# Scores and value products in one stretch each, and a new order of work on four engines, in a layered attention kernel

## The chip, the cores and the metric

The kernel runs on one core of a Trainium2 chip. The core has five engines that run their own instruction streams and meet only at semaphores: TensorE (PE for its matrix products, PEld for its weight loads), VectorE (DVE), ScalarE (ACT), GpSimd (POOL) and SyncE (SP, which issues the DMA transfers here). The metric is the device time of one execution in microseconds (us). Of the kernel before there are three runs, 1416.37, 1417.46 and 1418.73 us, and one profiled execution.

## The reference, cut to what matters

There are 16 sequences of 256 tokens with 256 channels. First comes a cross attention to a short context, then two layers of the kind below. The change touches the two layers alone.

```python
def _layer(x, wqkv, qs, ksc, wo, lg, lb, w1, b1, w2, b2):
    h = shift_token(x)                     # half of the channels come from the token before
    q, k, v = heads(h @ wqkv)              # 8 heads of 64
    q, k = rotary_xpos(l2norm(q) * qs, l2norm(k) * ksc)
    o = local_attention(q, k, v)           # windows of 128 tokens, each sees itself and the one before
    x = x + o @ wo
    h = layernorm(shift_token(x)) * lg + lb
    a, g = split(h @ w1 + b1)              # 2 * 682 columns
    return x + (a * gelu(g)) @ w2 + b2
...
x = x + xattn(layernorm(x), ctx)
x = x + ffn(layernorm(x))                  # two such layers
```

## The kernel before, in words

A step of the layer part handles one sequence of one layer, an item. There are 32 items, and the part is a pipeline written by hand: in step g the engines work on four items at once. In `run_l` they are called a (item g: projections to q, k and v, rotation and norms of q and k), b (item g-1: scores, softmax, value products, output projection), c (item g-2: layer norm and the hidden layer) and d (item g-3: the second product of the hidden layer). Steps 0 to 2 and 32 to 34 lack some of the four. Step 0 runs beside the end of the cross attention, step 33 and the rest finish the last item.

Every engine's `run_l` is a list of calls, and the order of that list is the order of its instructions. Nothing is scheduled by a tool. Each call waits on counters of the other engines (`at(b, 6, j)` is the count when piece j of item b is done), which guard data and also the reuse of the eight PSUM banks of `pb`; the tables `S_BANK`, `PT_BANK`, `QT_BANK`, `W1_BANK` say which bank a piece uses.

Names that matter here:

- `project(a, ..., t, part)`: six products of 512 columns, token tile t (0 or 1), part 0 q, 1 k, 2 v. `square` (ACT) and `squares` (DVE) form the norms, `rotate` (DVE) the two rotated parts, `add_parts`, `inverse_norms` and `norm_qk` (POOL) add them, take the inverse square root, and scale. `turn_qk` (PE) transposes the outcome and `copy_qk` (ACT) puts it into `qk_t`.
- `scores(..., j)`: j is 0, 1 or 2, and each makes two of the six softmax units u of item b. Their products have 64 rows (one head), and two heads share the array. `maxes` (DVE, with the mask), `exps` (ACT), `inverse_sums` and `norm_probs` (DVE, the division by the sum), `turn_p` (PE, transposes) and `probs_copy` (ACT) follow for each unit.
- `weigh(..., j)`: value products of units 2j and 2j+1, with 64 output columns each. `out_hi` (ACT) and `out_lo` (DVE) split the result into two parts, `out_product` (PE) multiplies by wo, `residual` (DVE) adds x. SP then moves one row down (`shift_down`), and `stats_h` (DVE) waits for that transfer.
- `turn_h`, `scale_h`, `split_h_hi`, `split_h_lo`, `hidden(..., m)`, `gelu`, `gate`, `gate_hi` (a cast), `gate_lo` (POOL): the hidden layer in six chunks m. `feed(..., k)` is its second product and `second_residual` adds it.
- `idle_products` are transposes whose result nobody reads. Before, 48 of them stand in step 1.

All matrix products but the scores, the value products and the transposes are sums of three products of parts (high and low), hence the threefold rows in the trace.

## Time and profile before

| | |
|---|---|
| median of 3 runs | 1417.46 us |
| the profiled execution's own time | 1418.17 us |
| its span, first to last instruction | 1416.2 us |
| granted clock of TensorE, mean | 0.999 |
| PE busy | 1384.4 us (98%) |
| PEld busy | 1239.3 us (88%) |
| DVE busy | 1097.6 us (78%) |
| ACT busy | 936.0 us (66%) |
| POOL busy | 783.8 us (55%) |

A row of the timeline reads: start, duration, engine, line, operation, output and inputs, shape, number of instructions, and in brackets the idle time ahead of it with what ended it. Products overlap, so the duration of one is longer than the distance to the next; what a product costs PE is the distance between the starts. A row of several instructions spans all of them. A row of the table by stretch reads: stretch, its length, busy time of PE, PEld, DVE, ACT and POOL with the number of instructions of each, the granted clock, the DMA engines' busy share, GB/s. Step 1 begins at 263.39 us, step 2 at 297.83, step 3 at 332.90, step 32 at 1362.08.

### The profile page before, as it was taken

How to read it: one execution, taken by the hardware profiler on the slowest of the kernel's cores; microseconds unless marked ns; L12 is line 12 of the kernel's file. 1: busy time of each engine (PE TensorE's matmuls, PEld its weight loads, DVE VectorE, ACT ScalarE, POOL GpSimd, SP SyncE). 2: the span in 40 equal slices, each digit the busy share in tenths (PEclk: the TensorE clock that was granted, in tenths of full speed). 3: DMA queues.
4: the chain of work that ended last, by engine and by line, in shares of the span. 5: the costliest groups of instructions: out<-in, count | busy, mean ns of one | idle time of the engine just before them, and what ended most of it. 6: DMA issues, size and time to landing. Idle time of an engine off the chain costs nothing.

```text
span 1416.2 us, 32821 instructions
## 1 busy us (share of the span) xinstructions
PE 1384.4 (98%) x11563; PEld 1239.3 (88%) x11563; DVE 1097.6 (78%) x3003; ACT 936.0 (66%) x2662; POOL 783.8 (55%) x640
## 2 busy tenths in 40 slices
PE   8999999989999999999999999999999999999998
PEld 7998998778888888888888888888888888888887
DVE  5777776668788788888888888788888888888874
ACT  6877767456666666666666667666666666666662
POOL 1212221646666666666666768766666666666643
PEclk9999999999999999999999999999999999999999
DMA  5223122101111001101111111111111111111101
GB/s 190 90 92 110 47 69 90 47 20 29 30 29 30 24 28 28 30 28 31 30 31 30 63 30 37 31 37 38 37 37 37 38 36 40 36 36 36 30 30 31
DMA packets 50517, 63.42 MB, mean 45 GB/s; under 512 B 8402, under 2 KB 32104, under 8 KB 50408
## 3 DMA queue, kind: packets, MB, share of 16 engines
q1 hardware_dynamic: 50408, 61.99, 14.0%
q8 instruction: 65, 1.06, 0.3%
q14 instruction: 44, 0.36, 0.1%
HBM read 38.17 MB, written 16.78 MB: 39 GB/s over the span
## 4 chain that ended last, share of the span: by engine, by line
PE 71%; DVE 12%; ACT 9%; issue 3%; DMA 2%; POOL 1%; SPq 1%; DVEq 0%; ACTq 0%; POOLq 0%
PE pb L568 34%; PE pb L881 7%; PE pb L895 6%; PE pb L857 6%; PE pb L826 6%; PE pb L841 5%; ACT x_p L1080 4%; PE pb L921 4%; ACT x_pt L1086 2%; DVE p_t L1593 1%; DMA x<-x 1%; DMA x_in<-x 1%; DVE p_t L1607 1%; DVE r_sin L1580 1%; ACT p_t L1223 1%
## 5 line engine op out<-in xcount | busy, mean ns | idle before, releaser
L1824 POOL TENSOR_TENSOR r_cos<-r_cos,r_sin 128x1024 f32<-128x1024 f32 x64 | 154.0, 2407 | 206.0 <-DVE r_sin L1580 206.0
L1223 ACT ACTIVATE p_t<-p_t,s_nm 128x128 f32<-128x128 f32 (+1 forms) x512 | 227.0, 445 | 25.9 <-DVE s_nm L1593 24.8
L568 PE MATMUL pb<-h_hi,w_hi 128*128 128x256 f32 x704 | 207.5, 295 | 1.5 <-DVE h_lo L1557 0.7
L568 PE MATMUL pb<-h_hi,w_lo 128*128 128x256 f32 x704 | 198.7, 282 | 0.0
L568 PE MATMUL pb<-h_lo,w_hi 128*128 128x256 f32 x704 | 198.6, 282 | 0.0
L1819 POOL TENSOR_TENSOR n_inv<-n_cl,half_neg 128x16 f32<-128x16 f32 x64 | 188.0, 2937 | 5.3
L1214 ACT ACTIVATE pt_t<-pb 128x512 f32<-128x512 f32 x192 | 113.8, 594 | 94.3 <-PE pb L841 93.8
L1607 DVE TENSOR_TENSOR p_t<-p_t,s_inv 128x512 f32<-128x512 f32 x192 | 173.4, 917 | 2.2
L568 PE MATMUL pb<-wqkv_hi,xt_hi 128*128 128x512 f32 x384 | 163.8, 427 | 3.6 <-DVE r_sin L1580 3.1
L1179 ACT ACTIVATE qk_sq<-pb 128x512 f32<-128x512 f32 x128 | 72.5, 592 | 142.9 <-PE pb L568 141.5
L1593 DVE CUSTOM_DVE_ANT_0 p_t<-pb,mask_t 128x128 f32<-128x128 f32 (+1 forms) x512 | 151.9, 353 | 16.9 <-PE pb L826 16.5
L1855 POOL TENSOR_TENSOR hg_lo<-hg,hg_hi 128x256 fp32r<-128x256 f32 (+1 forms) x192 | 142.1, 760 | 34.7 <-DVE hg_hi L1624 34.7
L568 PE MATMUL pb<-wqkv_lo,xt_hi 128*128 128x512 f32 x384 | 152.0, 396 | 0.0
L568 PE MATMUL pb<-wqkv_hi,xt_lo 128*128 128x512 f32 x384 | 150.7, 393 | 0.0
L568 PEld LDWEIGHTS pb<-h_hi,w_hi 128*128 128x128 f32 x704 | 134.0, 190 | 9.1 <-issue 6.4
L568 PEld LDWEIGHTS pb<-h_lo,w_hi 128*128 128x128 f32 x704 | 134.5, 191 | 0.0
L568 PEld LDWEIGHTS pb<-h_hi,w_lo 128*128 128x128 f32 x704 | 134.1, 191 | 0.0
L1831 POOL TENSOR_TENSOR r_cos<-r_cos,n_inv 128x1024 f32<-128x1024 f32 x64 | 123.4, 1929 | 5.0
L841 PE MATMUL pb<-ones_at,p_t 128*128 128x128 f32 x768 | 114.3, 279 | 5.0 <-DVE p_t L1607 4.3
L826 PE MATMUL pb<-qk_t 64*128 64x128 f32 (+1 forms) x1024 | 109.8, 343 | 1.3 <-DVE s_nm L1593 0.9
L1080 ACT ACTIVATE x_p<-pb,x_nm 128x77 f32<-128x77 f32 x256 | 79.2, 338 | 43.6 <-DVE x_nm L1375 43.6
L1202 ACT ACTIVATE gl<-pb,b_t 128x256 f32<-128x256 f32 x160 | 75.9, 475 | 46.3 <-PE pb L568 45.0
(145 smaller groups left out, 3920.7 us busy)
## 6 DMA issues: line engine op xcount, KB each, us to landing
y_state<-x SPq DMA_DIRECT2D x32, 256.0 KB, 2.0
x_cur<-y_state SPq DMA_DIRECT2D x32, 256.0 KB, 2.6
x_res<-y_state SPq DMA_DIRECT2D x32, 256.0 KB, 2.8
x_in<-x SPq DMA_DIRECT2D x16, 256.0 KB, 2.9
x_state<-x SPq DMA_DIRECT2D x16, 256.0 KB, 2.0
x_orig<-x_state SPq DMA_DIRECT2D x16, 256.0 KB, 2.9
out<-x SPq DMA_DIRECT2D x16, 256.0 KB, 2.2
x<-x SPq DMA_DIRECT2D x32, 112.0 KB, 2.3
```

What stands on the lines that cost most here:

```text
L568: mm = pe.matmul(dst, s, m, start=(n == 0 and k == 0), stop=(n == len(pairs) - 1 and k == 2))
L826: mm = pe.matmul(pb[:, S_BANK[u], k * keys:k * keys + keys], qk_t[r:r + DH, 0, ch, q_cols], qk_t[r:r + DH, 1, ch, 0:keys], start=True, sto ...
L841: mm = pe.transpose(pb[:, PT_BANK[u], k * P:k * P + P], p_t[:, u, k * P:k * P + P], id_f)
L1080: e = nc.scalar.activation(x_p[:, u, k, :], pb[:, 2 + u % 2, k * P:k * P + CTX], ACT.Exp, bias=x_nm[:, u, k:k + 1], scale=1.0, accum_out=x ...
L1214: nc.scalar.activation(pt_t[:, u % 4], pb[:, PT_BANK[u]], ACT.Copy).then_inc(act_pt, 1)
L1223: e = nc.scalar.activation(pu, pu, ACT.Exp, bias=s_nm[:, j, k:k + 1], scale=-1.0, accum_out=s_sum[:, j, k:k + 1])
L1593: e = nc.vector.tensor_tensor_reduce(p_t[:, j, k * keys:k * keys + keys], pb[:, S_BANK[j], k * keys:k * keys + keys], m, -1.0, FAR, ALU.ad ...
L1607: nc.vector.tensor_tensor(pu, pu, s_inv[:, u, 0:heads].unsqueeze(2).broadcast_to([P, heads, 512 // heads]), ALU.mult).then_inc(dve_pn, 1)
L1819: nc.gpsimd.tensor_tensor(n_inv[:, t], n_cl[:, t], half_neg[:], ALU.pow).then_inc(pool_inv, 1)
L1824: nc.gpsimd.tensor_tensor(r_cos[:, t], r_cos[:, t], r_sin[:, t], ALU.add).then_inc(pool_sum, 1)
L1831: nc.gpsimd.tensor_tensor(rows, rows, n_inv[:, t].unsqueeze(2).broadcast_to([P, 2 * HEADS, DH]), ALU.mult).then_inc(pool_qk, 1)
L1855: nc.gpsimd.tensor_tensor(hg_lo[0:rows, m], hg[0:rows, m], hg_hi[0:rows, m].bitcast(F32), ALU.subtract).then_inc(pool_hglo, 1)
```

## The change

It edits the order of the layer part on PE, ACT, DVE and POOL, with the banks and waits that go with it.

- PE: the three `scores` calls of a step stand directly behind each other, and so do the value products, now `weigh_late(0)`, `weigh_early`, `weigh_late(1)`. A step begins with `project(0, 1)`; `turn_next` and both halves of `out_product` move to the rear.
- `probs_copy` writes the transposed units back into `p_t` instead of a buffer of four (`pt_t` is gone), so `maxes` of the next item waits for the value products (`pe_av`) and no longer for the transposes.
- DVE, ACT, POOL: lists rewritten; `stats_h` goes from behind the second `maxes` to the rear of the step before. `gate(c, 0)` stands ahead of `rotate(a, 1)`.
- The idle products of step 1 are removed (16 in step 32 and 42 in step 0 stay), and the splitting of the second layer's wqkv goes in the order k, q, v.

```diff
-        S_BANK = [3, 4, 3, 4, 3, 4]
-        PT_BANK = [5, 7, 5, 7, 5, 2]
+        S_BANK = [2, 7, 3, 4, 5, 6]
+        PT_BANK = [5, 7, 5, 7, 4, 7]
...
+            def weigh_early(b, par):
+                pe.wait_ge(act_pt, at(b, UNITS, UNITS))
...
             def probs_copy(b, u):
                 act.wait_ge(pe_pt, at(b, UNITS, u + 1))
-                if u == 4:
-                    act.wait_ge(pe_av, at(b, 3, 1))
-                elif u in (0, 2) and later(b):
-                    act.wait_ge(pe_av, at(plus(b, -1), 3, 3 if u == 0 else 2))
-                nc.scalar.activation(pt_t[:, u % 4], pb[:, PT_BANK[u]], ACT.Copy).then_inc(act_pt, 1)
+                nc.scalar.activation(p_t[:, u], pb[:, PT_BANK[u]], ACT.Copy).then_inc(act_pt, 1)
...
# PE, run_l, a full step, new order (conditions left out)
+   project(0, 1); scores(0); scores(1); scores(2); project(0, 0)
+   feed(0); feed(1); turn_h; project(0, 2); feed(2); feed(3); feed(4)
+   turn_p(0); project(1, 0); feed(5); project(1, 1); project(1, 2)
+   turn_p(1); hidden(0); hidden(1); turn_p(2); turn_p(3); turn_p(4); hidden(2); turn_p(5)
+   weigh_late(0); weigh_early; weigh_late(1); hidden(3); turn_next
+   out_product(0); out_product(1); hidden(4); turn_qk(0); turn_qk(1); hidden(5); turn_qk(2); turn_qk(3)
...
# ACT, run_l, a full step, new order
+   square(0, 1); exps(0); exps(1); square(0, 0); scale_h; exps(2); copy_v(0); exps(3); exps(4)
+   probs_copy(0); square(1, 0); square(1, 1); exps(5); probs_copy(1); copy_v(1); gelu(0)
+   probs_copy(2) to (5); out_hi(0); gelu(1); out_hi(1); x_hi; gelu(2); gelu(3); gelu(4)
+   copy_qk(0); copy_qk(1); gelu(5); copy_qk(2); copy_qk(3)
...
# POOL, run_l, a full step, new order
+   gate_lo(d, 1) to (d, 4); deviation(c); gate_lo(d, 5); inverse_norms(0); add_parts(0); inverse_norms(1)
+   norm_qk(0); add_parts(1); kept_rows(c); gate_lo(c, 0); norm_qk(1)
```

On PE a step of before has three stretches of scores. The third stands between `feed` and `turn_p` (L881 and L841; L568 here the projections):

```order
L881 MATMUL pb<-w_hi,hg_hi 128x256
L881 MATMUL pb<-w_lo,hg_hi 128x256
L881 MATMUL pb<-w_hi,hg_lo 128x256
L826 MATMUL pb<-qk_t 128x128 x8
L841 MATMUL pb<-ones_at,p_t 128x128 x4
L568 MATMUL pb<-wqkv_hi,xt_hi 128x512
```

In the changed kernel all scores of a step stand between two projections (L840 scores, L571 the projections, L947 `turn_qk` of the step before):

```order
L947 MATMUL pb<-ones_at,r_cos 128x128 x8
L571 MATMUL pb<-wqkv_hi,xt_hi 128x512
L571 MATMUL pb<-wqkv_lo,xt_hi 128x512
L571 MATMUL pb<-wqkv_hi,xt_lo 128x512
L571 MATMUL pb<-wqkv_hi,xt_hi 128x512
L571 MATMUL pb<-wqkv_lo,xt_hi 128x512
L571 MATMUL pb<-wqkv_hi,xt_lo 128x512
L840 MATMUL pb<-qk_t 128x256 x8
L840 MATMUL pb<-qk_t 128x128 x8
L571 MATMUL pb<-wqkv_hi,xt_hi 128x512
```

Two changes of tile shape and back are gone from the step. (A row of the program is two in the trace for these products.)

The value products of before on PE, the first of their two stretches, with the transposes around it (L582 `turn_x`, L841 `turn_p`):

```order
L841 MATMUL pb<-ones_at,p_t 128x128 x8
L582 MATMUL pb<-ones_at,x_cur 128x128 x4
L857 MATMUL pb<-pt_t,v_t 64x128 x8
L841 MATMUL pb<-ones_at,p_t 128x128 x4
L568 MATMUL pb<-h_hi,w_hi 128x256
```

And in the changed kernel, one stretch behind the last `turn_p` (L857; L872 `weigh_late`, L884 `weigh_early`):

```order
L857 MATMUL pb<-ones_at,p_t 128x128 x4
L872 MATMUL pb<-p_t,v_t 64x128 x8
L884 MATMUL pb<-p_t,v_t 64x128 x8
L872 MATMUL pb<-p_t,v_t 64x128 x8
L571 MATMUL pb<-h_hi,w_hi 128x256
```

All of them now follow the last transpose, so the middle one has the copy of the last unit close ahead of it.

On DVE, before, the last division of a step follows the second rotation and the squares (L1574, L1580 `rotate`, L1563 `squares`, L1607 `norm_probs`):

```order
L1574 TENSOR_TENSOR r_cos<-pb,cos_t 128x512 [waits act_sq]
L1574 TENSOR_TENSOR r_cos<-pb,cos_t 128x512
L1580 TENSOR_TENSOR r_sin<-pb,sin_t 128x16x32 x2
L1563 TENSOR_REDUCE n_sq<-qk_sq 128x16 [waits pool_cl,act_sq]
L1601 RECIPROCAL s_inv<-s_sum 128x4 [waits act_exp]
L1607 TENSOR_TENSOR p_t<-p_t,s_inv 128x512 [waits dve_rec]
```

In the changed kernel the four last divisions (L1633) stand ahead of that rotation (L1600, L1606; L1589 `squares`):

```order
L1589 TENSOR_REDUCE n_sq<-qk_sq 128x16 [waits pool_cl,act_sq]
L1633 TENSOR_TENSOR p_t<-p_t,s_inv 128x512 [waits dve_rec] x2
L1627 RECIPROCAL s_inv<-s_sum 128x4 [waits act_exp] x2
L1633 TENSOR_TENSOR p_t<-p_t,s_inv 128x512 [waits dve_rec] x2
L1643 SCALAR_TENSOR_TENSOR hg<-pb,b_t,gl 128x256 [waits pool_hglo,act_gelu]
L1600 TENSOR_TENSOR r_cos<-pb,cos_t 128x512 [waits act_sq]
L1600 TENSOR_TENSOR r_cos<-pb,cos_t 128x512
L1606 TENSOR_TENSOR r_sin<-pb,sin_t 128x16x32 x2
```

So the divisions have moved ahead of the rotation, for which the sum of the rotated parts on POOL waits.

## Rows read from the trace of the kernel before

**Rows 1.** Busy by stretch: steps 1, 2, 3-31, one full step, step 32, 4 us.

```profile
263.39:297.83 34.44, 30.73 (x234) 25.66 (x232) 20.25 (x57) 18.07 (x53) 16.20 (x8) 0.95 0.08 26
297.83:332.90 35.07, 32.35 (x255) 27.32 (x255) 28.02 (x78) 22.06 (x60) 21.97 (x17) 1.00 0.08 20
332.90:1362.08 1029.18, 1024.21 (x8292) 915.15 (x8291) 836.35 (x2293) 686.36 (x1777) 664.89 (x500) 1.00 0.11 34
940.07:975.20 35.13, 35.13 (x287) 31.54 (x287) 28.84 (x79) 23.31 (x61) 22.47 (x18) 1.00 0.12 38
1362.08:1387.80 25.72, 22.29 (x205) 19.39 (x205) 14.91 (x56) 15.50 (x46) 2.53 (x4) 1.00 0.13 41
290.00:294.00 4.00, 4.00 (x33) 3.67 (x30) 1.29 (x2) 1.09 (x2) 2.77 (x2) 0.68 0.02 4
```

**Rows 2.** Timeline of PE around two stretches of scores in a full step.

```profile
945.34 0.28 PE L881 MATMUL pb<-w_hi,hg_lo 128*128 128x256 f32 x1
945.55 1.13 PE L826 MATMUL pb<-qk_t 64*128 64x256 f32 x8
946.61 0.50 PE L568 MATMUL pb<-wqkv_hi,xt_hi 128*128 128x512 f32 x1
946.95 0.40 PE L568 MATMUL pb<-wqkv_lo,xt_hi 128*128 128x512 f32 x1
...
951.72 1.16 PE L826 MATMUL pb<-qk_t 64*128 64x128 f32 x16
952.82 0.66 PE L841 MATMUL pb<-ones_at,p_t 128*128 128x128 f32 x4
```

**Rows 3.** Timeline of PE around the value products, and one copy on ACT.

```profile
957.63 0.60 PE L582 MATMUL pb<-ones_at,x_cur 128*128 128x128 f32 x4
958.16 1.09 PE L857 MATMUL pb<-pt_t,v_t 128*64 128x128 f32 x16
959.19 0.66 PE L841 MATMUL pb<-ones_at,p_t 128*128 128x128 f32 x4
...
964.41 0.60 PE L841 MATMUL pb<-ones_at,p_t 128*128 128x128 f32 x4
964.94 1.97 PE L857 MATMUL pb<-pt_t,v_t 128*64 128x128 f32 x32
966.84 0.39 PE L568 MATMUL pb<-h_hi,w_hi 128*128 128x256 f32 x1
...
965.04 0.60 ACT L1214 ACTIVATE pt_t<-pb 128x512 f32<-128x512 f32 x1
```

**Rows 4.** Timeline of DVE and POOL: divisions beside the power and beside the sum.

```profile
951.78 1.28 DVE L1607 TENSOR_TENSOR p_t<-p_t,s_inv 128x512 f32<-128x512 f32 x2
...
962.49 1.79 DVE L1607 TENSOR_TENSOR p_t<-p_t,s_inv 128x512 f32<-128x512 f32 x1
...
951.34 2.93 POOL L1819 TENSOR_TENSOR n_inv<-n_cl,half_neg 128x16 f32<-128x16 f32 x1
...
961.33 2.40 POOL L1824 TENSOR_TENSOR r_cos<-r_cos,r_sin 128x1024 f32<-128x1024 f32 x1 [4.93 <-DVE r_sin L1580]
```

**Rows 5.** Timeline of DVE: the residual and the statistics behind the shift.

```profile
940.17 0.69 DVE L1531 TENSOR_TENSOR x<-pb,x_res 128x512 f32<-128x512 f32 x1 [1.03 <-PE pb L895]
...
944.32 0.76 DVE L1537 BATCH_NORM_STATS2 l_st<-x 128x6 f32<-128x256 f32 x2 [1.44 <-DMA x<-x]
```

**Rows 6.** Groups by line and shape: maxes, rotation, squares, power, scaling.

```profile
L1819 POOL TENSOR_TENSOR n_inv<-n_cl,half_neg 128x16 f32<-128x16 f32 x64 | 188.0, 2937 | 5.3
...
L1831 POOL TENSOR_TENSOR r_cos<-r_cos,n_inv 128x1024 f32<-128x1024 f32 x64 | 123.4, 1929 | 5.0
...
L1593 DVE CUSTOM_DVE_ANT_0 p_t<-pb,mask_t 128x256 f32<-128x256 f32 x256 | 93.0, 420 | 16.6 <-PE pb L826 16.5
...
L1574 DVE TENSOR_TENSOR r_cos<-pb,cos_t 128x512 f32<-128x512 f32 x128 | 81.7, 680 | 3.3 <-ACT qk_sq L1179 3.1 <-issue 0.2
...
L1563 DVE TENSOR_REDUCE n_sq<-qk_sq 128x16 f32<-128x1024 f32 x64 | 77.6, 1213 | 0.0
```

More of the change, by code:

```diff
@@ L366, in qkv_bank @@
         def qkv_bank(a, t, part):
[L367 removed]
+            return (FIRST_BANK if is_first(a) else QKV_BANK)[t, part]
         def xt_bank(n):
@@ L941, in run_l @@
                     return
-                if isinstance(g, int) and g == 1:
-                    idle_products(5, 7)
+                if isinstance(g, int) and g == ITEMS:
+                    scores(a, b, c, d, 0)
+                    scores(a, b, c, d, 1)
+                    scores(a, b, c, d, 2)
+                    feed(b, c, d, 0)
+                    feed(b, c, d, 1)
+                    feed(b, c, d, 2)
+                    feed(b, c, d, 3)
+                    feed(b, c, d, 4)
+                    turn_p(a, b, d, 0)
+                    feed(b, c, d, 5)
+                    idle_products(16, 1)
+                    turn_h(b, c)
+                    turn_p(a, b, d, 1)
+                    hidden(a, b, c, 0)
+                    turn_p(a, b, d, 2)
+                    turn_p(a, b, d, 3)
+                    hidden(a, b, c, 1)
+                    turn_p(a, b, d, 4)
+                    turn_p(a, b, d, 5)
+                    weigh_late(a, b, c, was, 0)
+                    weigh_early(b, was)
+                    weigh_late(a, b, c, was, 1)
+                    hidden(a, b, c, 2)
+                    out_product(b, 0)
+                    out_product(b, 1)
+                    hidden(a, b, c, 3)
+                    hidden(a, b, c, 4)
+                    hidden(a, b, c, 5)
+                    return
@@ L984, in run_l @@
+                if c is not None:
+                    hidden(a, b, c, 2)
+                if b is not None:
+                    turn_p(a, b, d, 5)
+                if b is not None:
+                    weigh_late(a, b, c, was, 0)
+                    weigh_early(b, was)
+                    weigh_late(a, b, c, was, 1)
+                if c is not None:
+                    hidden(a, b, c, 3)
                 if has_next(a):
-                    turn_next(a, b, c)
+                    turn_next(a)
@@ L1259, in run_l @@
                     exps(b, 1)
+                if a is not None and not is_first(a):
+                    square(a, 0, 0)
+                if c is not None:
+                    scale_h(c, layer)
+                if b is not None:
                     exps(b, 2)
@@ L1309, in run_l @@
                     copy_qk(a, 1)
+                if c is not None:
+                    gelu(c, 5, layer)
+                    next_weights(g, 2)
+                if a is not None:
                     copy_qk(a, 2)
```

469 lines of the change are left out of this document (226 added, 243 removed).

## Prediction, on record before the changed kernel was run

> **What bounds the kernel now.** I first read the busy time by stretch [rows 1]. A full step takes 35.13 us and PE is busy in all of it, at full clock, while DVE has 28.84 us of work, ACT 23.31 and POOL 22.47. The 29 steps 3 to 31 take 1029.18 us; at 35.13 each they would take 1018.8, so 10.4 us are irregular waits. A step of the layers is therefore as long as PE's own list, and a gain must come out of what that list costs on PE, not out of a wait. Only steps 1 and 2 differ: step 1 lasts 34.44 us although it has neither hidden layer nor second product, and the clock is 0.95 in it, so it is made of waits and of idle products. Then I read PE's timeline for the distance between starts where the kind of product changes [rows 2, 3].
>
> **What a stretch of small tiles costs on PE.** Scores use 64 rows, value products 64 columns, all else the full array. Value products: 16 take 958.16 to 959.19, 1.03 us, and 32 take 964.94 to 966.84, 1.90 us [rows 3]. So 16 more cost 0.87, a pair 0.109, and every stretch has 0.16 us on top. Ahead of it four transposes take 0.53 us (957.63 to 958.16), where their own distance, (0.60 - 0.27) / 3 = 0.11, makes 0.44: 0.09 for the way in (0.27 is taken as the length of a single one). The first row behind lasts 0.66 against 0.60 for the same transposes elsewhere: 0.06 for the way out. Together 0.31 us for a stretch. Scores of 256 columns: four pairs at twice 0.109 would be 0.87, they take 1.06 (945.55 to 946.61), so 0.19; the way in is 945.34 to 945.55, 0.21 against about 0.12 for such a product (256 columns, half of the 0.23 to 0.24 of 512), 0.09; the first projection behind lasts 0.50 against 0.40, 0.10 [rows 2]. Together 0.38. The third stretch (128 columns, eight pairs) takes 1.10 against 0.87, 0.23, plus 0.09 and 0.06: 0.38.
>
> The change leaves one stretch of scores of three and one of value products of two. It saves 0.38 + 0.38 + 0.31 = 1.07 us a step. No product is added or taken out, and eight groups of transposes instead of seven cost nothing by rows: four take 0.44 with their way out. I put back 0.1 for what a change between the two score shapes may cost, which no row shows (between 0 and another 0.38). A full step then takes 35.13 - 0.98 = 34.15 us, if PE never waits.
>
> The Trainium skill says in "TensorEngine Tiling", section Key Properties, that changing the tiling mode drains TensorE while changing the tile alone does not. The 0.31 and 0.38 us are what this case's trace shows of it; by the page a switch between 64-row scores of two widths would cost nothing, which would make the step 34.05 us.
>
> **Does PE wait in the new order?** I laid the other engines' lists beside PE's new one, 0 being a step's first projection. PE then reaches scores at 1.6, the second projection at 4.4, `turn_h` 7.3, `turn_p(0)` 11.3, `turn_p(1)` 16.2, hidden 16.6, `turn_p(5)` 22.3, values 22.8 to 25.6, `out_product` 27.5 to 30.4, `turn_qk` 31.8.
>
> - Divisions on DVE. A division beside POOL's power takes 0.64 (two in 1.28 us, 951.78, POOL busy 951.34 to 954.27); beside the sum it takes 1.79, and it ends 0.55 after the sum does (962.49 to 964.28, sum until 963.73) [rows 4]. So the full-width POOL operations hold DVE's division or cast back until they end, the narrow power does not. In the new order DVE does the first division and the split of h while POOL does the power of tile 0, and four divisions in the power of tile 1. The second one follows the rotation without a break, so DVE starts it before POOL has seen the rotation. 1.1 us of blocking goes, but off PE's path.
> - DVE from the first maxes at 2.9: five maxes 3.6 us (0.35 for each of 256 keys, 0.42 with its end), `norm_h` 0.65, squares 1.15, two divisions 1.2, split 1.1, rotation 2.4 (four of 0.60), residual 0.6, last maxes 0.9, and 0.6 of reciprocals and waiting, 12.2 in all (maxes, squares and rotation by [rows 6], divisions by [rows 4], the others set equal to their like). It ends at 15.1, hidden needs it at 16.6: 1.5 spare.
> - The last unit: `turn_p(5)` starts at 22.3; its copy ends 1.3 later (before: 964.41 to 965.64, 1.23). `weigh_early` comes 0.53 for the transposes and 0.9 for the first 16 value rows later, 1.4. Some 0.15 spare, the tightest place.
> - POOL's last scaling: squares of tile 1 end at 16.8, power and clamp 3.7, scaling 1.9, sum 2.4 (after a wait for the rotation), kept rows and one `gate_lo` 2.1, scaling 1.9: 29.4 against 31.8.
> - ACT copies the last q/k tile by 0.8 of the next step; scores need it at 1.6.
> - The statistics, now at DVE's rear, wait for the shift. The residual starts at 31.7 at the latest, and from its start to the statistics it was 4.15 us (940.17 to 944.32) [rows 5]: 35.9, which is 1.7 of the next step, plus 1.0 of work: 2.7, just ahead of the maxes at 2.9. Nothing is lost.
>
> So steps 3 to 31 take 29 x 34.15 = 990.4 us, plus irregular waits. Half of the old 10.4 us stays, I estimate, since the long waits there fall where the new order has 1 us of spare, but the split of wqkv and w1 now stands ahead of work that is late: 5 us. 995.4 against 1029.18: -33.8.
>
> **Steps 1, 2 and 32.** In step 1 PE waits for others. New order: first division 8.5 us in, projections of tile 1 end at 13.2, squares of tile 1 at 13.8; then POOL alone is the chain: clamp and power 3.7, scaling 1.93, sum 2.4, scaling 1.93 [rows 4, 6], 23.8, and 16 transposes 1.8: 25.7 us against 34.44, -8.7. In the old order the last division stands behind a rotation, squares and the sum, and the second `out_product` behind everything. Step 2 lacks the second product, 32 x 0.12 = 3.8 us, and waits 1.4 us for its first division: 31.8 against 35.07, -3.3. Step 32 has no projection: scores wait 1.1 us for the q/k copies and, since `scale_h` stands ahead of `exps(2)` on ACT, the softmax waits for `turn_h` at 10. The residual comes 28.5 us in and not 26.0: +2.5. What is behind it keeps its length.
>
> **Sum.** 1418.17 - 33.8 - 8.7 - 3.3 + 2.5 = 1374.9 us, by the profiled execution, which is 0.7 above the median of the runs. I forecast 1375 us, -3.0%.
>
> **Rivals.**
>
> - A short wait in every step, at the value products (0.15 spare) or at the scores (0.8 spare). For: the two smallest margins, and no row shows the copies in this order. 0.3 to 0.6 us a step, 29 times: 1384 to 1392.
> - Joining saves only part: the 0.19 and 0.23 us inside a stretch are not its beginning but the pace of its pairs. For: the pair at 256 columns is only inferred. Then 0.42 us a step less is gained, 1387, and with a wait on top up to 1400.
> - The clock. Without the 48 idle products PE of step 1 pauses some 1 us at a time. The clock was 0.68 in 290 to 294 [rows 1], behind a pause of 2.5 us; there the row of 32 value products took longer than its 1.97. At half clock for 4 us the loss is 2 us: 1377. The skill's page "TensorE: Matmul & The Clock Gate", section What's actually happening, says that an idle engine falls to the lower level; the trace agrees at that place.
> - **Slower: the statistics at DVE's rear become the loop.** Shift, statistics, maxes, ..., last maxes, hidden, `out_product`, residual, shift is a closed ring through every step. It has 0.2 + 1.5 = 1.7 us of spare at a shift of 3.5 us. Each us beyond lengthens all steps. Break-even is a step of 35.64 us (29 x 35.64 + 5 = 1029.18 + 9.5), a shift of 6.7 us. At 7.2, from other transfers of SP beside it, a step is 36.15 and the time 1433. For: DVE idles for this transfer in every step now. Against: 3.5 us [rows 5].
> - **Slower by a rule.** If POOL's power of 2.94 us [rows 6] blocked DVE as the sum does, the split of h in the new order would end 3.2 us late, hidden 1.7 us late, a step would take 35.85, and the time would be 1424. Divisions take 0.64 us beside it [rows 4], so no. The skill's "SBUF — State Buffer", section SBUF: two separate sides, says that whichever of a GpSimd operation and a VectorE one with two SBUF inputs starts first holds the shared ports to its end; the trace agrees for the sum, not for the power.
> - The order moves but the step stays 35.1: only steps 1, 2 and 32 gain, 1409.
>
> **How the numbers follow.** Forecast 0.58 (1366 to 1384), short wait 0.18, joining saves part 0.09, clock 0.04, step stays 0.03, ring 0.05, rule 0.01, 0.02 for anything else that ends within 0.2%. Range 1364 to 1398: below, both open costs at nothing and no irregular wait; above, into part-saving with a wait. 0.2% is about what the runs can tell from no change. Faster 0.92, same 0.02, slower 0.06.
>
> **What would show it.** Right: a full step of 34.1 to 34.3 us, PE busy in all of it; one row of scores of some 2.8 us and one of value products of 2.8; step 1 near 26 us, step 32's residual 28 us in. Wrong: idle time of PE ahead of `weigh_early` on ACT's copy, or ahead of hidden on the maxes; DVE idle at the statistics for more than 1 us; a division of 1.7 us; a row of scores of 3.2 us.

## The result and the profile after

| | before | after |
|---|---|---|
| median of the runs | 1417.54 us (1416.37 to 1418.73, 4 runs) | 1372.26 us (1371.82 to 1373.79, 4 runs) |
| ratio after : before | | 0.9686, 95% interval 0.9675 to 0.9698 |
| span of the profiled execution | 1416.2 us | 1371.6 us |
| granted clock, mean | 0.999 | 0.996 |
| PE busy | 1384.4 us | 1343.5 us (98%) |
| DVE busy | 1097.6 us | 1033.0 us (75%) |
| POOL busy | 783.8 us | 797.3 us (58%) |

The change makes the kernel 3.1% faster, 45 us; the forecast was 1375 us. The table by stretch answers [rows 1]: length of the stretch, then busy time of PE, PEld, DVE, ACT and POOL, granted clock, DMA share, GB/s. The stretches are step 1, step 2, steps 3 to 31, one full step, step 32 up to the last residual, and the last residual to the end.

```profile
263.54:289.55 26.01, 23.35 (x187) 19.21 (x185) 18.60 (x59) 17.53 (x53) 15.70 (x8) 1.00 0.13 34
289.55:321.75 32.20, 30.78 (x257) 27.53 (x256) 26.48 (x77) 22.07 (x62) 22.40 (x16) 1.00 0.09 24
321.75:1315.08 993.33, 990.60 (x8293) 914.89 (x8292) 776.01 (x2295) 689.39 (x1779) 678.90 (x499) 1.00 0.12 35
973.30:1007.42 34.12, 34.12 (x289) 31.55 (x288) 26.57 (x80) 23.51 (x62) 22.98 (x17) 1.00 0.13 38
1315.08:1342.71 27.63, 23.83 (x218) 22.69 (x219) 14.34 (x57) 16.11 (x47) 2.86 (x4) 0.94 0.10 33
1342.71:1371.60 28.89, 21.68 (x164) 20.93 (x162) 14.61 (x34) 5.28 (x11) 10.88 (x15) 0.94 0.13 38
```

Steps 3 to 31 gave 35.9 us (1029.18 to 993.33), step 1 8.4, step 2 2.9. The last part, from the scores of step 32 to the end, lasts 56.5 us against 54.1: 2.4 lost. 25 of the 29 steps last 34.12 us, each PE's list without a pause; step 18 lasts 36.79 and holds most of what is irregular. Of the 35.9 us, 29 x 1.01 = 29.3 are the shorter full step; the other 6.6 are irregular waits that went (10.4 before, 3.8 now).

PE's timeline of that full step, at the places of [rows 2, 3]. Columns: start, length, engine and line, operands, tile and shape, count.

```profile
974.87 2.89 PE L840 MATMUL pb<-qk_t 64*128 64x256 f32 x32
977.69 0.50 PE L571 MATMUL pb<-wqkv_hi,xt_hi 128*128 128x512 f32 x1
...
995.49 0.60 PE L857 MATMUL pb<-ones_at,p_t 128*128 128x128 f32 x4
996.02 1.09 PE L872 MATMUL pb<-p_t,v_t 128*64 128x128 f32 x16
996.94 1.04 PE L884 MATMUL pb<-p_t,v_t 128*64 128x128 f32 x16
997.82 1.04 PE L872 MATMUL pb<-p_t,v_t 128*64 128x128 f32 x16
998.79 0.38 PE L571 MATMUL pb<-h_hi,w_hi 128*128 128x256 f32 x1
```

One stretch of scores, 974.87 to 977.69, 2.82 us; before, the same 32 products took 1.06 + 1.06 + 1.10 = 3.22 in three. One stretch of value products, 2.77 against 1.03 + 1.90. The rest of the 1.01 us, 0.45, lies in the products just ahead of a stretch and just behind it, of which there are now fewer.

DVE and POOL in the same step, which answers [rows 4]:

```profile
981.73 0.68 DVE L1633 TENSOR_TENSOR p_t<-p_t,s_inv 128x512 f32<-128x512 f32 x1
...
990.02 1.28 DVE L1633 TENSOR_TENSOR p_t<-p_t,s_inv 128x512 f32<-128x512 f32 x2
...
982.01 0.79 POOL L1841 TENSOR_SCALAR n_cl<-n_sq 128x16 f32<-128x16 f32 x1 [4.96 <-DVE n_sq L1589]
982.88 3.38 POOL L1843 TENSOR_TENSOR n_inv<-n_cl,half_neg 128x16 f32<-128x16 f32 x1
986.24 2.50 POOL L1848 TENSOR_TENSOR r_cos<-r_cos,r_sin 128x1024 f32<-128x1024 f32 x1
```

No division is held in this step, and in the whole run only two of the 192 are (one takes 2.57 us, in step 18). Their mean fell from 917 to 697 ns, 192 x 0.22 = 42 of the 64.6 us that DVE is busy less. The price is on POOL, whose power takes 3.38 us here against 2.93, and 3213 ns in the mean against 2937 [rows 6]. What decides is what DVE does when the power begins: it takes 3.20 us in all 31 cases in which it begins inside a division, 3.32 to 3.39 inside the split of h (`h_lo`), 2.98 inside the cast ahead of it, and 2.93 otherwise. PE is busy in all of the full step before and after, so neither shows in its length. Groups of the page (busy us, mean ns of one, idle before):

```profile
L1843 POOL TENSOR_TENSOR n_inv<-n_cl,half_neg 128x16 f32<-128x16 f32 x64 | 205.6, 3213 | 5.3
...
L1633 DVE TENSOR_TENSOR p_t<-p_t,s_inv 128x512 f32<-128x512 f32 x192 | 128.5, 697 | 0.0
```

DVE's residual and, at the start of the next step, the statistics, which answer [rows 5]. The statistics stand ahead of all maxes now and wait 0.80 us for the shift; the full step stays PE's own list:

```profile
1004.43 0.68 DVE L1557 TENSOR_TENSOR x<-pb,x_res 128x512 f32<-128x512 f32 x1
1008.61 0.76 DVE L1563 BATCH_NORM_STATS2 l_st<-x 128x6 f32<-128x256 f32 x2 [0.80 <-DMA x<-x]
```

### The profile page after: what moved, and what is told of

Read it like the earlier page. It is cut to its first block, busy times and chain, and to the rows that moved or that the text cites. A ratio compares the mean times of both kernels' runs of the same rounds, so it can differ in the third digit from the quotient of the medians.

```text
span 1371.6 us, 32716 instructions
## 1 busy us (share of the span) xinstructions
PE 1343.5 (98%) x11515; PEld 1236.5 (90%) x11515; DVE 1033.0 (75%) x3003; ACT 938.3 (68%) x2662; POOL 797.3 (58%) x640
## 3 DMA queue, kind: packets, MB, share of 16 engines
q8 instruction: 65, 1.06, 0.3%
## 4 chain that ended last, share of the span: by engine, by line
PE 79%; ACT 7%; DVE 6%; POOL 4%; issue 2%; DMA 2%; SPq 0%; POOLq 0%; DVEq 0%
PE pb L571 38%; PE pb L909 8%; PE pb L840 7%; PE pb L923 6%; PE pb L857 6%; PE pb L872 4%; PE pb L947 4%; ACT x_p L1112 4%; PE pb L884 2%; ACT x_pt L1118 2%; DMA x_in<-x 1%; POOL n_inv L1843 1%; PE pb L796 1%; PE pb L585 1%; POOL r_cos L1855 1%
## 5 line engine op out<-in xcount | busy, mean ns | idle before, releaser
L571 PE MATMUL pb<-h_hi,w_hi 128*128 128x256 f32 x704 | 210.0, 298 | 1.2 <-DVE h_lo L1583 0.9
L1843 POOL TENSOR_TENSOR n_inv<-n_cl,half_neg 128x16 f32<-128x16 f32 x64 | 205.6, 3213 | 5.3
L571 PE MATMUL pb<-h_hi,w_lo 128*128 128x256 f32 x704 | 199.0, 283 | 0.0
L571 PE MATMUL pb<-h_lo,w_hi 128*128 128x256 f32 x704 | 199.0, 283 | 0.0
L1848 POOL TENSOR_TENSOR r_cos<-r_cos,r_sin 128x1024 f32<-128x1024 f32 x64 | 157.8, 2465 | 14.3 <-DVE r_sin L1606 13.8
L571 PE MATMUL pb<-wqkv_hi,xt_hi 128*128 128x512 f32 x384 | 162.8, 424 | 0.2 <-DVE xt_lo L1374 0.2
L1643 DVE SCALAR_TENSOR_TENSOR hg<-pb,b_t,gl 128x256 f32<-128x256 f32 (+1 forms) x192 | 91.8, 478 | 87.8 <-ACT gl L1234 65.3
L571 PE MATMUL pb<-wqkv_lo,xt_hi 128*128 128x512 f32 x384 | 152.1, 396 | 0.0
L571 PE MATMUL pb<-wqkv_hi,xt_lo 128*128 128x512 f32 x384 | 150.4, 392 | 0.0
L1841 POOL TENSOR_SCALAR n_cl<-n_sq 128x16 f32<-128x16 f32 x64 | 38.6, 603 | 188.2 <-DVE n_sq L1589 188.1
L1234 ACT ACTIVATE gl<-pb,b_t 128x256 f32<-128x256 f32 x160 | 72.5, 472 | 100.4 <-PE pb L571 100.0
L571 PEld LDWEIGHTS pb<-h_hi,w_hi 128*128 128x128 f32 x704 | 134.1, 190 | 7.1 <-issue 5.7
L1242 ACT ACTIVATE p_t<-pb 128x512 f32<-128x512 f32 x192 | 106.9, 591 | 40.7 <-PE pb L857 40.3
L571 PEld LDWEIGHTS pb<-h_lo,w_hi 128*128 128x128 f32 x704 | 134.7, 191 | 0.0
L571 PEld LDWEIGHTS pb<-h_hi,w_lo 128*128 128x128 f32 x704 | 134.2, 191 | 0.0
L1633 DVE TENSOR_TENSOR p_t<-p_t,s_inv 128x512 f32<-128x512 f32 x192 | 128.5, 697 | 0.0
L1211 ACT ACTIVATE qk_sq<-pb 128x512 f32<-128x512 f32 x128 | 76.3, 596 | 57.4 <-PE pb L571 55.7
L857 PE MATMUL pb<-ones_at,p_t 128*128 128x128 f32 x768 | 106.0, 274 | 7.3 <-DVE p_t L1633 3.7
```

The source lines that it names most:

```text
L571: mm = pe.matmul(dst, s, m, start=(n == 0 and k == 0), stop=(n == len(pairs) - 1 and k == 2))
L857: mm = pe.transpose(pb[:, PT_BANK[u], k * P:k * P + P], p_t[:, u, k * P:k * P + P], id_f)
L1242: nc.scalar.activation(p_t[:, u], pb[:, PT_BANK[u]], ACT.Copy).then_inc(act_pt, 1)
L1633: nc.vector.tensor_tensor(pu, pu, s_inv[:, u, 0:heads].unsqueeze(2).broadcast_to([P, heads, 512 // heads]), ALU.mult).then_inc(dve_pn, 1)
L1843: nc.gpsimd.tensor_tensor(n_inv[:, t], n_cl[:, t], half_neg[:], ALU.pow).then_inc(pool_inv, 1)
L1848: nc.gpsimd.tensor_tensor(r_cos[:, t], r_cos[:, t], r_sin[:, t], ALU.add).then_inc(pool_sum, 1)
```

## The experiments

All medians are to be read beside 1372.26 us (changed) and 1416.4 to 1417.6 us (before, on the same chips). Lengths of steps are from one profiled execution of each kernel.

### 1. Scores taken apart again

```
                     scores(a, b, c, d, 1)
-                    scores(a, b, c, d, 2)
                 if a is not None and not is_first(a):
                     project(a, b, c, d, 0, 0)
+                if b is not None:
+                    scores(a, b, c, d, 2)
```

> The changed kernel with its scores taken apart again: the third pair of score units stands behind the step's second projection, so that there are two stretches of score products in each of the 31 steps that have scores and a projection, instead of one. Theory (a stretch of tiled products costs TensorE 0.28 to 0.38 us, since rows 128 and 256 wide cost the same pitch per column in one stretch): each full step 34.12 -> 34.40 to 34.50 us, the whole 1372.3 -> 1381 to 1384 us, with no new wait of TensorE. Rival (joining bought nothing, and the 1.0 us a step came from waits that went): within 1 us of 1372.3.

1383.31 us, +11.0, as the theory said and against the rival. The full step went to 34.53, +0.41, a little more than expected, without a wait:

```profile
945.62 2.00 PE L840 MATMUL pb<-qk_t 64*128 64x256 f32 x16
947.55 0.50 PE L571 MATMUL pb<-wqkv_hi,xt_hi 128*128 128x512 f32 x1
...
949.14 1.16 PE L840 MATMUL pb<-qk_t 64*128 64x128 f32 x16
950.23 0.39 PE L909 MATMUL pb<-w_hi,hg_hi 128*128 128x256 f32 x1
```

1.93 and 1.09 us from start to start against 2.82 joined: 0.20 inside, and as much in the larger products at the borders. A stretch of scores costs 0.41 us here.

### 2. Value products taken apart again

```
                     weigh_late(a, b, c, was, 0)
-                    weigh_early(b, was)
-                    weigh_late(a, b, c, was, 1)
                 if c is not None:
                     hidden(a, b, c, 3)
+                if b is not None:
+                    weigh_early(b, was)
+                    weigh_late(a, b, c, was, 1)
```

> The changed kernel with its value products taken apart: the late half's first 16 products, then the fourth hidden chunk, then the other 32 products. One stretch more in each of 31 steps, or 30 with a hidden chunk between. Theory (0.31 us a stretch): each full step 34.12 -> 34.43 us, the whole 1372.3 -> 1381.5 us, and up to 0.1 us a step more if the output product, which now comes about 0.1 us behind its remainders instead of 1.3 us, has to wait (then up to 1385). Rival (joining bought nothing): within 1 us of 1372.3.

1393.07 us, +20.8, twice what was expected. The full step is 34.63 us, +0.51. PE:

```profile
1008.65 1.09 PE L872 MATMUL pb<-p_t,v_t 128*64 128x128 f32 x16
1009.68 0.38 PE L571 MATMUL pb<-h_hi,w_hi 128*128 128x256 f32 x1
...
1011.30 1.09 PE L884 MATMUL pb<-p_t,v_t 128*64 128x128 f32 x16
...
1013.20 0.66 PE L585 MATMUL pb<-ones_at,x_cur 128*128 128x128 f32 x4
1013.82 0.39 PE L923 MATMUL pb<-wo_hi,o_hi 128*128 128x256 f32 x1
```

The two stretches take 1.03 and 1.90 us, 2.93 against 2.77 joined: 0.16. The way into the second one adds 0.09 (1011.09 to 1011.30 where such a product takes 0.12). The transposes behind it take 0.62 us up to the next product, against 0.36 in the changed kernel (1000.32 to 1000.68): 0.26, which makes the 0.51. But 0.62 is not the price of transposes behind value products. In the kernel before, four such transposes stand right behind value products too, and take 0.41 us (959.19 to 959.60, first row below), 0.05 more than 0.36. The other 0.21 is a wait, which PE's own rows hide because its products overlap, and which its weight loads show (the other rows, of this run):

```profile
959.60 0.36 PE L568 MATMUL pb<-h_hi,w_hi 128*128 128x256 f32 x1
...
1013.07 0.69 DVE L1664 TENSOR_TENSOR o_lo<-pb,o_hi 128x512 fp32r<-128x512 f32 x1 [4.09 <-ACT o_hi L1258]
...
1013.81 0.19 PEld L923 LDWEIGHTS pb<-wo_hi,o_hi 128*128 128x128 f32 x1 [0.20 <-DVE o_lo L1664]
```

`out_product` waits for DVE's remainder `o_lo`, which ends at 1013.76. In this run PEld has 32 such waits, 7.6 us together; in the changed kernel it has one, of 0.2. So the stretch itself costs 0.30 us (0.31 forecast), and the other 0.21 is the wait that the expectation had put at 0.1 at most: what stood between the value products and `out_product` had been its cover. 29 x 0.51 is 14.8; steps 3 to 31 together lost 17.6, and steps 2 and 32 another 1.9. What goes beyond 0.51 a step falls in steps 2, 16, 18, 19, 31 and 32, most of which wait in the changed kernel too; it was not traced further.

### 3. The kernel before without its idle products of step 1

```
-                if isinstance(g, int) and g == 1:
-                    idle_products(5, 7)
...
-                    idle_products(26, 4)
```

(and the groups of 6 and 11)

> The kernel before without the 48 idle transposes of step 1 (5, 6, 26 and 11); its order of work and all its waits stay. Theory (step 1 waits for chains of other engines, which the idle products only fill, and the 8.4 us of step 1 came from the new order): step 1 stays at 34 to 34.5 us and the whole at 1416 to 1418 us. Rival A (the 48 products were themselves the time: 48 x 0.107 us): step 1 29 to 30 us, the whole 1412 to 1413. Rival B (without them the clock falls): granted clock below 0.9 between 263 and 298 us and the whole 1418 to 1424.

1415.86 us, ratio 0.9992 (0.9983 to 1.0001): no difference. Windows: step 1 from its scores on, and 290 to 300.

```profile
264.63:300.51 35.88, 27.35 (x185) 22.43 (x185) 20.25 (x57) 17.12 (x51) 16.20 (x8) 0.86 0.07 22
290.00:300.00 10.00, 8.58 (x65) 8.18 (x62) 1.29 (x2) 3.15 (x6) 3.01 (x2) 0.62 0.01 2
```

The idle products were not the time, so rival A is out. Without them the clock falls to 0.62 (0.87 with them in the same 10 us) and the step, 33.44 us from its scores on with them, takes 35.88. So the theory held for the total and missed step 1, and rival B was right on the clock and wrong on the total: steps 3 to 31 took 1026.76 us in this profile and not 1029.18, which takes the 2.4 us of step 1 back. Why is open. Taking the idle products out gave nothing by itself, so the 8.4 us of step 1 came from the new order. There the clock stays at 1.00 without them; PE's longest pause in that step is now 1.16 us.

### 4. GpSimd's order of before in the changed kernel

```
-                    inverse_norms(a, 0)
...
-                    add_parts(a, 0)
-                    inverse_norms(a, 1)
...
-                    norm_qk(a, 0)
-                    add_parts(a, 1)
...
-                    norm_qk(a, 1)
+                    rotated(a, 0)
+                    rotated(a, 1)
```

(`kept_rows` and `gate_lo` then follow; the three splits of the second layer's w1 and wo stand ahead of both)

> The changed kernel with GpSimd's work on queries and keys in the order of before: for each half sum, clamp, power and scaling in one chain, instead of clamp and power first and the scaling of the first half ahead of the second sum. Theory (GpSimd's order is not mere cover: its last scaling ends at 1002.9 against TensorE's turn of queries and keys at 1005.0, and the chain makes it 2.4 + 4.0 + 1.9 us behind the second rotation, which ends at 996.4 to 997.2): last scaling at 1005 to 1006, TensorE waits 0.2 to 0.8 us in each full step, the whole 1372.3 -> 1378 to 1397 us. Rival (the spare of 2.1 us holds, and GpSimd's order costs nothing): within 2 us of 1372.3.

1385.59 us, +13.3, inside the range I gave, but for another reason: the full step stayed at 34.12 us, as the rival said.

```profile
1000.62 0.24 POOL L1841 TENSOR_SCALAR n_cl<-n_sq 128x16 f32<-128x16 f32 x1
1000.95 2.93 POOL L1843 TENSOR_TENSOR n_inv<-n_cl,half_neg 128x16 f32<-128x16 f32 x1
...
1008.13 2.36 POOL L1848 TENSOR_TENSOR r_cos<-r_cos,r_sin 128x1024 f32<-128x1024 f32 x1 [1.94 <-DVE r_sin L1606]
...
1013.80 1.91 POOL L1855 TENSOR_TENSOR r_cos<-r_cos,n_inv 128x1024 f32<-128x1024 f32 x1
```

The last scaling ends 30.7 us into the step (985.01) and PE needs it at 31.7: 1.0 of spare. In the full steps GpSimd's new order is cover. What the old one costs is 3.8 us in step 1, 1.4 in step 32 and 8.3 in steps 3 to 31, 5.1 of them in step 18, where the splits of the weights, now in one piece, hold DVE's normalization back (PE waits 5.2 us at `turn_h`). Step 1 is a clean case. PE's timeline:

```profile
286.65 0.28 PE L923 MATMUL pb<-wo_hi,o_lo 128*128 128x256 f32 x1
290.12 3.22 PE L947 MATMUL pb<-ones_at,r_cos 128*128 128x128 f32 x16 [3.19 <-POOL r_cos L1855]
```

In the changed kernel that wait is 0.59 us and the 16 transposes last 1.97, not 3.22; behind the long wait the granted clock of 290 to 293 is 0.61. So 3.8 of step 1's 8.4 us are GpSimd's order, clock included; which of the other moves gave the other 4.6 was not tested one at a time.

### 5. Residual rows ahead of the shift

```
                     sp.wait_ge(dve_x1, at(c, 1, 1))
-                    shift_down(c)
                     if b is not None:
                         sp.dma_start(x_res[:], ...)
+                    shift_down(c)
```

> The changed kernel with SyncE's load of the residual rows (196 KB) issued ahead of the shift of the attention result, not behind it, in every step. So the shift lands later; in the changed kernel it lands 3.4 to 3.7 us behind the end of the residual. Theory (the ring of shift, statistics, maxes, hidden products and residual has 1.7 us of spare in every step): the shift lands 0.5 to 1.5 us later, the statistics start so much later, the full step stays at 34.12 us and the whole within 2 us of 1372.3, but for step 32 and the end, where the shift is on the path (+0 to +3). Rival (the ring has no spare, the statistics set the step): each us of delay makes each of 29 steps as much longer, 1387 to 1415 us.

1374.44 us (ratio 0.9699, 0.9682 to 0.9716; the changed kernel's is 0.9675 to 0.9698). From the residual's end to the statistics it is now mostly 3.97 us, not 3.5 (the load is 256 KB by the page, not 196). The full steps stay at 34.12. Such a delay is too small to say how much spare there is beyond it.

### 6. turn_h early in step 32

```
                     feed(b, c, d, 1)
+                    turn_h(b, c)
                     feed(b, c, d, 2)
...
                     feed(b, c, d, 5)
-                    idle_products(16, 1)
-                    turn_h(b, c)
+                    idle_products(8, 1)
```

> The changed kernel with one edit in step 32 alone: the turn of the normalized rows stands behind the second feed product instead of behind the sixth, and 8 idle transposes stand where 16 did. Theory (ScalarE's scaling of the turned rows, and behind it the exponentials of units 2 to 4, wait for this turn until 1324.7, though the rows are ready at 1319.2; DVE's divisions and the second residual wait for them, and TensorE pauses 3.8 us): the turn comes at 1320, the pause shrinks to 0 to 1 us, step 32 takes 23.5 to 24.5 us instead of 27.6, the whole 1368 to 1369 us. Rival (the pause only moves: DVE's second residual or last maxes bind anyway): 1371 to 1373 us.

1368.04 us, 4.2 less than the changed kernel; step 32 takes 22.87 us instead of 27.63. The changed kernel, PE and ACT:

```profile
1324.10 0.60 PE L796 MATMUL pb<-ones_at,h_n 128*128 128x128 f32 x4
1328.30 0.63 PE L857 MATMUL pb<-ones_at,p_t 128*128 128x128 f32 x4 [3.59 <-DVE x L1657]
...
1324.74 1.02 ACT L1221 ACTIVATE h_n<-pb,lnb_t,lng_t 128x256 f32<-128x256 f32 x2 [5.42 <-PE pb L796]
```

and this run:

```profile
1319.46 0.60 PE L796 MATMUL pb<-ones_at,h_n 128*128 128x128 f32 x4
...
1323.96 0.63 PE L857 MATMUL pb<-ones_at,p_t 128*128 128x128 f32 x4 [0.19 <-DVE x L1657]
...
1320.10 1.02 ACT L1221 ACTIVATE h_n<-pb,lnb_t,lng_t 128x256 f32<-128x256 f32 x2 [0.80 <-PE pb L796]
```

ACT's idle time of 5.42 us ahead of `scale_h` was the cause of PE's wait on the second residual, further down the lists of ACT and DVE. The edit also takes out 8 idle transposes (1.91 us for 16, 1.04 for 8). PE now waits only 0.19 us for that residual, so with all 16 it would reach the place up to 0.7 us late: that much of the 4.8 may be theirs, which no run separates.

### 7. Two more edits in the last steps

```
-                    deviation(l_mv[:, :, 1], l_ve[:], ..., b, ...)
                     gate_lo(c, gate_chunks(c)[1])
+                    deviation(l_mv[:, :, 1], l_ve[:], ..., b, ...)
```

(on top of experiment 6; and, in step 31 alone, `hidden(5)` and `gelu(5)` behind all of `turn_qk` and `copy_qk`)

> As the run before, and two edits more: in step 31 the last hidden chunk stands behind all turns of queries and keys, so that ScalarE's last copies have it as cover (now the scores of step 32 wait 0.8 to 1.0 us for them); at the end of step 32 GpSimd makes the remainder of the second gate chunk ahead of the statistics' deviation, not behind it, so that the second feed product of the last steps doesn't wait from 1347.0 to 1349.9. Theory: 0.8 us from the first and 0.5 to 1.0 us from the second on top of the earlier turn, 1366.5 to 1367.5 us. Rival (each only moves the wait; the chain of residual, shift, statistics and norm sets the end): as the run before, 1368 to 1369 us.

1367.79 us, the ratio 0.9647 of experiment 6 again, and not the 1366.5 to 1367.5 expected. Steps 31 and 32 together last 57.62 us against 57.57: the wait for the copies became one of 0.7 us at the first feed product, for DVE's maxes, which stand behind the statistics. The other edit shortened the part behind the last residual from 28.67 to 27.71 in the profiles, but the medians don't tell it apart.

### 8. A weight split earlier in step 18

```
+                if isinstance(g, int) and g == SEQS + 2:
+                    next_w1(0)
                 if c is not None and not (isinstance(g, int) and g == ITEMS + 1):
                     deviation(l_mv[:, :, 1], l_ve[:], l_rs[:], c, ...)
```

(on top of experiment 7; its old place further down is empty)

> As the run before, and in step 18 GpSimd splits the first third of the new layer's weights ahead of the statistics' deviation, when it idles, instead of behind it. There DVE's normalization of 2 x 0.43 us took 2.43 us, from 840.1 to 842.5, while GpSimd's split ran until 842.0, and TensorE waited 1.1 us. Theory (DVE's operation with both operands in SBUF waits for GpSimd's full-width one, so the order of the two decides): the normalization takes 0.8 us, the wait of TensorE at the turn goes, 1.0 to 1.2 us less than the run before, 1365.5 to 1366.5 us. Rival (no blocking; the normalization was late for another reason): no difference beyond 0.3 us to the run before.

1367.33 us (ratio 0.9643, 0.9625 to 0.9660), the fastest here, but not told apart from 6 and 7 by the medians. The local effect is plain. The changed kernel, DVE, POOL and PE:

```profile
840.07 2.43 DVE L1571 TENSOR_SCALAR h_n<-x,l_mv,l_rs 128x256 f32<-128x256 f32 x2
...
839.64 2.38 POOL L1891 TENSOR_TENSOR w_lo<-raw_a,w_hi 128x1024 fp32r<-128x1024 f32 x1
...
842.56 0.66 PE L796 MATMUL pb<-ones_at,h_n 128*128 128x128 f32 x4 [0.97 <-DVE h_n L1571]
```

and this run, where PE has no such wait:

```profile
840.06 0.72 DVE L1575 TENSOR_SCALAR h_n<-x,l_mv,l_rs 128x256 f32<-128x256 f32 x2
...
835.55 2.37 POOL L1895 TENSOR_TENSOR w_lo<-raw_a,w_hi 128x1024 fp32r<-128x1024 f32 x1 [1.83 <-ACT w_hi L1075]
```

The same normalization takes 0.72 us once GpSimd's split is over, as the theory said. Step 18 falls from 36.36 (experiment 7) to 35.80, 0.56 and not the 1.0 to 1.2 expected: PE's wait at this place was only 0.6 us in experiment 7.

### 9. Joining alone, in the kernel before

```
-        S_BANK = [3, 4, 3, 4, 3, 4]
+        S_BANK = [3, 4, 5, 6, 3, 4]
...
                     scores(a, b, c, 0)
+                    scores(a, b, c, 1)
```

(the second pair waits for the residual, the third for the first two maxes; the second one's old place is empty)

> The kernel before with one part of the change alone: the first two of its three stretches of score products stand together at the step's start, in four banks instead of two (the second pair waits for the residual instead of for the first maxes). Nothing else moves. Theory (a stretch costs TensorE 0.38 us wherever it stands): 31 stretches fewer, the full step 35.13 -> 34.75 us, the whole 1417.0 -> 1405 us, a quarter of the change's 45 us. Rival (in the kernel before, the time saved comes back as a wait, because the rest of its order is late too): 1410 to 1420 us.

1438.12 us, ratio 1.0145 (1.0123 to 1.0167): slower by 21.5, against both theories. ACT and DVE of a full step that starts at 1093.12:

```profile
1098.36 1.09 ACT L1181 ACTIVATE qk_sq<-pb 128x512 f32<-128x512 f32 x2 [5.75 <-PE pb L568]
...
1100.76 0.51 ACT L1225 ACTIVATE p_t<-p_t,s_nm 128x256 f32<-128x256 f32 x1
...
1099.48 1.29 DVE L1576 TENSOR_TENSOR r_cos<-pb,cos_t 128x512 f32<-128x512 f32 x2 [0.80 <-ACT qk_sq L1181]
```

Before, ACT's squares began 4.16 us into the step, the exponentials at 6.56, the rotation at 5.32; here it is 5.24, 7.64 and 6.36. The joined scores put the two projections 1.0 us later, and everything behind them in the lists of ACT and DVE slid by as much. Most full steps rose from 35.13 to between 35.83 and 36.12. PE waits in 31 steps, 11.8 us in all (3.1 us in 5 before), for DVE's rotation at its first projection of tile 1 (experiment 12 returns to it). And the joined stretch took 2.07 us, hardly less than twice 1.06, where experiment 1 has 1.93 without a wait: DVE's residual ends at 1094.07, and the second eight products start at 1094.13, behind it.

### 10 and 11. The shift held back

```
                     sp.wait_ge(dve_x1, at(c, 1, 1))
-                    shift_down(c)
                     if b is not None:
                         sp.dma_start(x_res[:], ...)
+                    if d is not None and b is not None:
+                        sp.wait_ge(dve_hghi, at(d, FC, 5))
+                    shift_down(c)
```

(11: `pool_hglo` in place of `dve_hghi`)

> The changed kernel with SyncE holding the shift back, in each step, until the rounding of the fifth gate chunk is done, 1.45 us behind the end of the residual (the load of the residual rows goes first). The shift then lands some 1.5 us later than in the changed kernel. Theory (the ring of shift, statistics, maxes, hidden products, output product and residual has 1.7 us of spare): nothing in the full steps, 34.12 us, and only the last steps lengthen by 1 to 2 us: 1372 to 1376 us. Rival (no spare): 29 x 1.5 us, 1415 us.

1380.37 us. From residual to statistics it is 4.5 to 5.1 us in most steps, 1.1 to 1.7 more than in the changed kernel. Of the full steps most stay at 34.12, steps 4 to 6 among them with 1.6 to 1.7 us of delay, but seven take 0.2 to 0.3 more and steps 14, 18 and 19 take 0.9 to 1.5 more, so that steps 3 to 31 lost 5.1 us together. Step 2 lost 1.0, the last part 1.7. The forecast of 1372 to 1376 missed these.

> As the run before, but held until GpSimd's remainder of the fifth gate chunk, 2.3 us behind the end of the residual. Theory (1.7 us of spare): 0.4 to 0.8 us in each of 29 full steps, 34.5 to 34.9 us, the whole 1384 to 1397 us. Rival A (more spare than 1.7, since DVE's later work has waits that absorb it): full steps at 34.12 and 1373 to 1377 us. Rival B (no spare): 29 x 2.3 us, 1439 us.

1407.46 us, more than the 1384 to 1397 expected. Here it is 5.5 us, 2.0 more. The shortest full steps take 34.43 to 34.48, some +0.34; most of the others alternate between 34.6 and 35.1 to 35.2. DVE, then PE (in brackets the idle time before, and what ended it):

```profile
1067.53 0.75 DVE L1565 BATCH_NORM_STATS2 l_st<-x 128x6 f32<-128x256 f32 x2 [2.98 <-DMA x<-x]
...
1070.99 0.36 PE L911 MATMUL pb<-w_hi,hg_hi 128*128 128x256 f32 x1 [0.79 <-DVE s_nm L1621]
```

By the steps that lose least, the two bracket the spare: at up to 1.7 us of delay nothing, at 2.0 a loss of 0.34, so about 1.7 us, as forecast. Some of the long steps fit it: in step 5 of this run the statistics came 7.2 us behind the residual, 3.8 more than in the changed kernel, and the step lost 2.1. But the ring closes elsewhere than I had put it. Not the hidden layer waits for the last maxes, but the first feed product for the first ones, which stand behind the statistics on DVE. In all the trace puts 17.3 us in 21 waits down to that place. The whole loss of steps 3 to 31 is 29.0 us, where 29 x 0.34 would be 9.9. The rest lies in the longer steps. Why every second one is longer at the same delay was not settled, so 1.7 us is the spare of the best steps and not of all.

### 12. Joining with two orders changed

```
+                    exps(b, 0)
+                    exps(b, 1)
                 if a is not None and not is_first(a):
                     square(a, 0, 0)
                     square(a, 0, 1)
...
                     maxes(b, 1)
+                    maxes(b, 2)
+                    maxes(b, 3)
                 if c is not None:
                     stats_h(c)
```

(on top of experiment 9; each added call left its later place)

> The run with the two stretches of scores joined in the kernel before (1438 us, slower by 21), with two orders changed as well. There the joined scores put the first projections 1.06 us later; ScalarE's squares wait for these, and its exponentials stand behind the squares; DVE's rotation waits for the squares, and its maxes of units 2 and 3 stand behind the rotation. Now ScalarE makes the exponentials of units 0 and 1 ahead of the two squares, and DVE the maxes of units 2 and 3 ahead of statistics and rotation. Theory (joining pays only where the other engines' lists are rearranged with it; the 1.0 us a step lost there was this delay handed on): full steps from 35.85 to 36.09 back to 34.8 to 35.1 us, the whole 1405 to 1417 us. Rival (the joined scores cost more on TensorE itself, by their wait for the residual or by bank traffic): full steps stay above 35.6 us, the whole above 1430.

1431.42 us, ratio 1.0098 (1.0082 to 1.0115): 6.7 of the 21.5 us came back; most full steps take 35.55 to 35.84. The theory's 1405 to 1417 fails. The rival's numbers hold (above 1430, and most full steps above 35.6). Of its two reasons the trace shows the banks, as a wait and not as traffic. PE still waits in 31 steps, 12.2 us in all, at one place, as it did in experiment 9:

```profile
PE pb L568 <- DVE r_sin L1583: 12.2, 31, 2.3
```

That is the first projection of tile 1. It writes the bank out of which DVE still rotates tile 0, and the rotation starts 6.37 us into the step, as late as in experiment 9 (6.36): neither of the two changed orders moved it. The change takes this away by its table of banks: there that projection has bank 2 and waits for the copy of the value part, done at 983.72 where the projection starts at 984.94. So the kernel before needs three things beside the join: ACT's order, DVE's order, and free banks. That the three are enough is argued from the changed kernel, which has them all and other moves too, and not shown by undoing them one at a time.

## Why the prediction was right

- **The bound.** A full step is PE's own list, before and after. Shown: PE busy 34.12 of 34.12 us, and 35.13 of 35.13 before.
- **The price of a stretch.** Forecast 1.07 us for two stretches of scores and one of value products, less 0.1 put back; measured 1.01. Experiment 1 gives 0.41 for a stretch of scores (0.38 forecast), experiment 2 gives 0.30 for one of value products (0.31 forecast), and 0.21 for a wait of `out_product` beside it. The 0.1 for the change of width was not needed as such: in the joined row the 256-column scores start 0.216 us apart, the first 128-column one 0.216 behind the last of these, and the rest 0.11 apart. Without it the terms give 1.07, 0.06 more than was measured, and where these 0.06 lie is open.
- **No wait in the new order.** Forecast checkpoints against measured, from 973.30: `turn_h` 7.3 and 7.30, `turn_p(0)` 11.3 and 11.29, hidden 16.6 and 16.5, `turn_p(5)` 22.3 and 22.19, `turn_qk` 31.8 and 31.74. The last maxes end at 15.2 (15.1). The statistics are done at 2.0 of this step and 2.4 of the next, not 2.7, since the residual starts at 31.1 and not at 31.7. The tightest place, 0.15 at `weigh_early`, held: ACT's copy ends at 996.72, the products start at 996.94.
- **Irregular waits of steps 3 to 31.** 5 us forecast, as half of the old ones; 993.33 - 29 x 34.12 = 3.8. No row stood behind the half, and which move took which wait away was not tested.
- **Steps 1 and 2.** 25.7 and 31.8 forecast, 26.01 and 32.20 measured. GpSimd's chain is the one that ends last in step 1: PE's transposes wait for its last scaling. The clock, a rival with 0.04, did not fall there; it fell in step 32 (0.94, and 1.00 before), where a pause of 3.6 us was left.
- **Step 32.** The term was +2.5 us up to the residual. Measured from the scores, the residual comes 27.63 us in and not 26.03 (1362.08 to 1388.11 before), +1.6, the wait of 0.8 for the copies ahead of the scores is counted in step 31, and behind the residual another 0.8 was lost, where the prediction had said that this part keeps its length. That 1.6 and 0.8 make the 2.4 beside a term of 2.5 is therefore luck in part. Its reason, `scale_h` ahead of `exps(2)` on ACT, is shown by experiment 6, which takes 4.8 us off step 32.
- **The slower rival.** The ring's spare of 1.7 us is right in size for the steps that lose least (10, 11) and wrong in place: feed, not hidden.
- **The blocking rule.** By the Trainium skill's "SBUF — State Buffer", section SBUF: two separate sides, whichever of a GpSimd operation and a VectorE one with two SBUF inputs or in a two-port mode starts first holds the shared ports to its end. The trace agrees for GpSimd's full-width split ahead of DVE's normalization (2.43 against 0.72 us, experiment 8), and for DVE's divisions ahead of the power (3.20 against 2.93). It does not agree for the power ahead of divisions: two of them beside it take 1.28 us.
- **The sum.** Forecast were -33.8, -8.7, -3.3 and +2.5 us; measured are -35.9, -8.4, -2.9 and +2.4. So the terms hold one by one, but for the luck named under step 32.
- **What I underrated.** The prediction reads as if joining carried the 1 us a step and the other orders were there not to spoil it. That is true as arithmetic of PE's list, and experiment 9 shows how much hangs on the second half: the join alone, with the banks and waits that it needs, costs 21 us.

## What to carry to other kernels

Where one engine is busy in all of a step, look at what its list costs where the kind of product changes: each stretch of tiled products had a price of 0.3 to 0.4 us here, with its borders, and joining them gives that back. But a join moves everything behind it later, so work out first who waits for the work that it is put ahead of, by engine order and by bank. A join of two stretches of scores was worth 11 us in the new order (experiment 1) and lost 21 in the old one (experiment 9). And look at what covers a wait before you move it: in experiment 2 a hidden chunk left its place between the value products and `out_product`, and 0.21 us a step came back as a wait. And give the steps at the ends of the pipeline an order of their own: one call moved in the last attention step, with 8 idle products less, was worth 4.2 us.
